# Four chained attention layers: values of two layers from one product, weights turned in one piece, output in quadrants

## The reference, cut to what matters

```
# layer 1, decay
w = exp(-exp(time_decay + tanh(xw @ td_w1) @ td_w2))        # td_w1: 256x64, td_w2: 64x256
# layer 2
v      = h_lojban @ w_v.T                                    # context
probs  = softmax(q @ k.T / sqrt(256))
x2     = x1 + alpha * (probs @ v) @ w_o.T
# layer 3
v      = encoder_hidden_state @ Wv + bv                      # the same context, 64 columns
out    = softmax(scores) @ v
```

## Time and profile before

| | |
|---|---|
| median of 3 runs | 1621.43 us (1621.12 to 1624.65) |
| span of the profiled execution | 1618.4 us |
| outside the span, against the median | 3.0 us |
| TensorE, VectorE, ScalarE, GpSimd busy | 88%, 67%, 38%, 39% |
| one full iteration | 92.4 to 92.9 us, a few of them 94 to 96 |

### The profile page before, as it was taken

One profiled execution on the slowest core, in us unless ns is written; L12 is line 12 of the kernel. 1 busy time (PEld: TensorE's weight loads), 2 busy tenths in 40 slices (PEclk: granted clock), 3 DMA queues, 4 the chain that ended last, 5 costly groups with the idle time before them and its releaser, 6 DMA issues.

```text
span 1618.4 us, 34489 instructions
## 1 busy us (share of the span) xinstructions
PE 1416.4 (88%) x14312; PEld 1073.0 (66%) x14312; DVE 1076.6 (67%) x2073; ACT 622.2 (38%) x1351; POOL 626.3 (39%) x604
## 2 busy tenths in 40 slices
PE   5878999999999999999999999999999999987664
PEld 4656777666777776666777766667777667765443
DVE  2354686866768686776868677686868667774735
ACT  2333444334334443434444443444443343432221
POOL 1061615336261634526162543616153352605210
PEclk9898999999999999999999999999999999997786
DMA  7030313114031312304041221403131130404000
GB/s 288 11 56 14 57 31 46 39 24 71 17 57 31 53 33 33 60 17 63 25 63 31 40 44 23 72 17 57 32 45 40 29 65 17 54 4 57 3 11 7
DMA packets 65787, 70.40 MB, mean 43 GB/s; under 512 B 19808, under 2 KB 54752, under 8 KB 65248
## 3 DMA queue, kind: packets, MB, share of 16 engines
q1 hardware_dynamic: 65632, 68.19, 22.1%
HBM read 30.42 MB, written 4.19 MB: 21 GB/s over the span
## 4 chain that ended last, share of the span: by engine, by line
PE 61%; DVE 15%; ACT 8%; POOL 6%; issue 4%; DMA 4%; SPq 1%; DVEq 0%; POOLq 0%; ACTq 0%
PE pw L411 13%; PE pw L389 12%; PE pw L591 7%; PE pw L597 7%; PE pw L447 4%; PE pw L542 4%; DMA big<-kvrg 4%; PE pw L495 3%; DVE c L1096 3%; PE pw L395 2%; ACT ptA L814 2%; PE pw L400 2%; POOL ab L1039 2%; DVE ab L1250 2%; POOL ab L1003 1%
## 5 line engine op out<-in xcount | busy, mean ns | idle before, releaser
L1250 DVE TENSOR_TENSOR_SCAN ab<-pw,ab 128x256 f32<-128x256 f32 x256 | 160.4, 674 | 107.0 <-ACT ab L924 81.3
L1003 POOL TENSOR_TENSOR ab<-big,kvrg 128x504 f32<-128x504 f32 x128 | 161.5, 1262 | 74.3 <-DMA big<-kvrg 50.9
L1039 POOL TENSOR_TENSOR ab<-ab,kvrg 128x512 f32<-128x512 f32 x128 | 167.7, 1315 | 0.5 <-DVE ab L1250 0.5
L988 POOL TENSOR_TENSOR vtmp_B<-mv_B,eps 128x2 f32<-128x2 f32 x16 | 3.1, 197 | 383.7 <-DVE mv_B L1111 383.7
L1026 POOL TENSOR_TENSOR big<-big,xaB 128x512 f32<-128x512 f32 x80 | 93.3, 1175 | 99.8 <-DVE big L1229 99.8
L389 PE MATMUL pw<-big,wb 128*128 128x256 f32 x512 | 127.8, 393 | 0.2 <-ACT kvrg L897 0.2
L591 PE MATMUL pw<-tA,wb 128*128 128x256 f32 x512 | 125.5, 396 | 2.1 <-DVE tA L1194 2.1
L1229 DVE SCALAR_TENSOR_TENSOR big<-pw,wa,sxB 128x256 f32<-128x256 f32 x160 | 67.0, 478 | 78.1 <-PE pw L495 78.1
L816 ACT ACTIVATE ptC<-pw 128x1024 f32<-128x1024 f32 x64 | 62.1, 1022 | 146.8 <-PE pw L447 146.8
L597 PE MATMUL pw<-wb,ptA 128*128 128x256 f32 x512 | 115.6, 379 | 0.0
L591 PEld LDWEIGHTS pw<-tA,wb 128*128 128x128 f32 x512 | 97.9, 196 | 25.0 <-issue 9.3
(11 more groups left out here) (211 smaller groups left out, 3096.8 us busy)
## 6 DMA issues: line engine op xcount, KB each, us to landing
big<-kvrg SPq DMA_DIRECT2D x256, 128.0 KB, 3.9
hT<-in_h SPq DMA_DIRECT2D x16, 512.0 KB, 4.1
wb<-in_wb SPq DMA_DIRECT2D x1, 5120.0 KB, 21.2
a<-in_x SPq DMA_DIRECT2D x16, 256.0 KB, 2.7
xB<-in_x SPq DMA_DIRECT2D x16, 256.0 KB, 2.7
result<-c SPq DMA_DIRECT2D x16, 256.0 KB, 2.0
m<-in_mask SPq DMA_DIRECT2D x16, 128.0 KB, 2.5
m<-in_amask SPq DMA_DIRECT2D x32, 64.0 KB, 2.3
```

Of the source, the lines that this page charges most:

```text
L1003: G.tensor_tensor(ab[i % 4][:, :, :, 1:S], vx[i % 3].rearrange("p j (b s) -> p j b s", b=NB)[:, :, :, 0:S - 1], k, ALU.mult).then_inc(kv_p ...
L1039: G.tensor_tensor(ab[i % 4][:, :, :, :], st[i % 2][:, :, :, :], r, ALU.mult).then_inc(pd_ok, 1)
L1250: last = V.tensor_tensor_scan(st[i % 2][:, j, :, :].rearrange("p b s -> p (b s)"), kn(b5)[:, i // 4, :], ab[i % 4][:, j, :, :].rearrange(" ...
```

## The change

Three edits.

1. `v3` is no longer a stage. `m_vo` is 64 columns wider and carries layer 3's value weights; `l2v` makes 320 columns for each sequence, into two banks (sequences 0 and 2 or 1 and 3 in one), and ScalarE copies both to `uS`. VectorE takes layer 3's values out of `uS` (SBUF) into `v3s`, in eight pieces as before, but at stage `l2v`, so ahead of `fv`. The load of the next context moves from `v3` to `k3`.
2. `l2p` is one transpose of 128x128; `l2o` takes weights and values of token tile c from partitions 64c on, writes sequence e of it to partitions 64e on, and each token tile to a bank of its own.
3. `td2` is stored twice with 128 rows (once in the upper half, once in the lower, zeros elsewhere); `pw1`'s tanh is one instruction of 128 rows, and `pw2` is four products of 128 rows and 128 columns.

```diff
-ORDER = "ABABBABBBABBABBCBABBABBBBBCACBCBBBCCABBCCACBCBBBCAAACBBBBCABCBACAABCAABBCACCCACCC"
+ORDER = "ABABBABBBABBABBCBABBABBBBBCACBCBBBCCABBCCACBCBBBCAAABBBBCABCBACAABCAABBCACCCACCC"
...
-USES = {... "l2v": 1, ... "l2o": 1, "k3": 1, "v3": 1, ...}
+USES = {... "l2v": 2, ... "l2o": 2, "k3": 1, ...}
...
@@ TensorE
                 elif name == "pw2":
                     for m in range(2):
-                        last = mm(kn(b5)[:, m, :], w("td2")[0:64, m * P:(m + 1) * P], thB[0:64, 0, :], start=True, stop=True)
+                        for c in range(TT):
+                            last = mm(kn(b5)[:, m, tok(c)], w("td2", c)[:, m * P:(m + 1) * P], thB[:, 0, 0:P], start=True, stop=True)
...
                 elif name == "l2v":
-                    for b in range(NB):
-                        g = slice(64 * (b % 2), 64 * (b % 2) + 64)
+                    for kk in (k, k + 1):
+                        if kk > k and kk >= FIRST_FREE:
+                            pe.wait_ge(*spare(kk))
                         for c in range(2):
-                            last = mm(kn(bank(k))[g, b // 2, :], hT[t % 3][:, c, b, 0:S], m_vo[:, c, :], start=(c == 0), stop=(c == 1))
-                    last.then_inc(full(k)[0], 1)
+                            for h in range(2):
+                                last = mm(bank(kk)[64 * h:64 * h + 64, 0:C + 64], hT[t % 3][:, c, 2 * h + kk % 2, 0:S], m_vo[:, c, :],
+                                          start=(c == 0), stop=(c == 1))
+                        last.then_inc(full(kk)[0], 1)
...
                 elif name == "l2p":
-                    for c in range(TT):
-                        for e in range(2):
-                            g = slice(64 * e, 64 * e + 64)
-                            last = mm(bank(k)[g, c * S:(c + 1) * S], pbd[g, c, :], ident[g, g], start=True, stop=True)
-                    last.then_inc(full(k)[0], 1)
+                    nc.tensor.transpose(bank(k)[:, 0:P], pbd.rearrange("p t n -> p (t n)"), ident).then_inc(full(k)[0], 1)
                 elif name == "l2o":
+                    pe.wait_ge(*spare(k + 1))
...
                     for c in range(TT):
+                        g = slice(64 * c, 64 * c + 64)
                         for e in range(2):
-                            g = slice(64 * e, 64 * e + 64)
-                            last = mm(kn(bank(k))[g, c, :], ptb[g, c, :], uS[g, c, :], start=True, stop=True)
-                    last.then_inc(full(k)[0], 1)
+                            last = mm(bank(k + c)[64 * e:64 * e + 64, 0:C], ptb[g, e, :], uS[g, e, 0:C], start=True, stop=True)
+                        last.then_inc(full(k + c)[0], 1)
...
@@ ScalarE
                 elif name == "l2v":
-                    A(flat(uS), bank(k)[:, :], ACT.Copy).then_inc(read(k)[0], 2)
+                    for kk in (k, k + 1):
+                        if kk > k:
+                            act.wait_ge(*full(kk))
+                        A(uS[:, kk % 2, :], bank(kk)[:, 0:C + 64], ACT.Copy).then_inc(read(kk)[0], 2)
...
@@ VectorE
-                elif name == "v3":
-                    k = SLOT[name, i, t]
-                    dve.wait_ge(*full(k))
-
+                elif name == "l2v":
+                    dve.wait_ge(*read(SLOT[name, i, t]))
+                    dve.wait_ge(*read(SLOT[name, i, t] + 1))
                     for e in range(2):
                         for h in range(2):
                             for v in range(2):
                                 o = (2 * v + e) * W3
-                                last = V.tensor_copy(v3[64 * e:64 * e + 64, h:NB:2, :, v, o:o + W3],
-                                                     bank(k)[64 * h:64 * h + 64, 0:P].rearrange("p (b r x) -> p b r x", b=2, r=2)[:, :, :, o:o + W3])
-                    last.then_inc(read(k)[0], 2)
+                                last = V.tensor_copy(v3[64 * e:64 * e + 64, 2 * h:2 * h + 2, :, v, o:o + W3],
+                                                     uS[64 * h:64 * h + 64, :, C:C + 64].rearrange("p b (r x) -> p b r x", r=2)[:, :, :, o:o + W3])
+                    last.then_inc(v3_ok, 1)
...
@@ VectorE, once
-                V.tensor_scalar(flat(m_vo[:, :, :]), b5[:, :], vec("alpha"), None, ALU.mult).then_inc(set_m, 1)
+                V.tensor_copy(m_vo[:, :, C:C + 64], w("v3").rearrange("p (k n) -> p k n", k=2))
+                V.tensor_scalar(m_vo[:, :, 0:C], kn(b5), vec("alpha"), None, ALU.mult).then_inc(set_m, 1)
```

More of the change, by code:

```diff
@@ L36 @@
 WEIGHTS_B = [("w1", 2 * HID), ("w2", 8 * C),
-             ("m1", 2 * 160), ("m2", 2 * C), ("td1", 2 * 64), ("td2", C),
+             ("m1", 2 * 160), ("m2", 2 * C), ("td1", 2 * 64), ("td2", 2 * C),
              ("wk", 2 * C), ("wv", 2 * C), ("wr", 2 * C), ("wg", 2 * C), ("wo", 2 * C),
@@ L74 @@
     + [("gnorm", 0), ("gnorm", 1), ("gnorm", 2), ("gnorm", 3), ("gturn", 0), ("outg", 0), ("norm2", 0)],
-    "C": [(n, 0) for n in ("cturn", "fk", "l2k", "fr", "l2v", "fv", "x2turn", "l2s", "l2p", "l2o", "k3", "v3", "x3turn", "q3")]
+    "C": [(n, 0) for n in ("cturn", "fk", "l2k", "fr", "l2v", "fv", "x2turn", "l2s", "l2p", "l2o", "k3", "x3turn", "q3")]
     + attention(1) + [("norm3", 0)],
@@ L78 @@
 AHEAD = {"A": 2, "B": 1, "C": 0}
-ORDER = "ABABBABBBABBABBCBABBABBBBBCACBCBBBCCABBCCACBCBBBCAAACBBBBCABCBACAABCAABBCACCCACCC"
-USES = {"q0": 1, "k0": 2, "v0": 2, "out0": 1, "zturn": 2, "up": 1, "down": 1, "cturn": 2, "fk": 1, "l2k": 1, "fr": 1, "l2v": 1, "fv": 1,
-        "x2turn": 1, "l2s": 1, "l2p": 1, "l2o": 1, "k3": 1, "v3": 1, "x3turn": 1, "q3": 1, "out1": 1}
+ORDER = "ABABBABBBABBABBCBABBABBBBBCACBCBBBCCABBCCACBCBBBCAAABBBBCABCBACAABCAABBCACCCACCC"
+USES = {"q0": 1, "k0": 2, "v0": 2, "out0": 1, "zturn": 2, "up": 1, "down": 1, "cturn": 2, "fk": 1, "l2k": 1, "fr": 1, "l2v": 2, "fv": 1,
+        "x2turn": 1, "l2s": 1, "l2p": 1, "l2o": 2, "k3": 1, "x3turn": 1, "q3": 1, "out1": 1}
 RING = 2
@@ L164, in build @@
         m_qk = sb("m_qk", [P, 2, C])
-        m_vo = sb("m_vo", [P, 2, C])
+        m_vo = sb("m_vo", [P, 2, C + 64])
         qb0m = sb("qb0m", [P, 2, 2])
@@ L226, in build @@
         c3 = sb("c3", [P, TT, C])
-        fkS, kkS, gC, tS, uS, thC = (ptC[:, 512 * i:512 * (i + 1)].rearrange("p (k n) -> p k n", k=2) for i in range(6))
+        fkS, kkS, gC, tS, thC = (ptC[:, 512 * i:512 * (i + 1)].rearrange("p (k n) -> p k n", k=2) for i in (0, 1, 2, 3, 6))
+        uS = ptC[:, 2048:2048 + 2 * (C + 64)].rearrange("p (k n) -> p k n", k=2)
         pbd, ptb = (ptC[:, 3584 + 128 * i:3712 + 128 * i].rearrange("p (t n) -> p t n", t=TT) for i in range(2))
@@ L303, in build @@
         gn_d, gn_p, gt_ps, gt_sb, og_ok, og_ps = sem("gn_d"), sem("gn_p"), sem("gt_ps"), sem("gt_sb"), sem("og_ok"), sem("og_ps")
-        kk_ok, ff_d, l2_mx = sem("kk_ok"), sem("ff_d"), sem("l2_mx")
+        kk_ok, ff_d, l2_mx, v3_ok = sem("kk_ok"), sem("ff_d"), sem("l2_mx"), sem("v3_ok")
         fin_ok = sem("fin_ok")
@@ L354, in stage @@
                     load_x(t + 2, xB[t % 2], ld_x4[t % 2])
-                elif name == "v3" and t + 3 < TILES:
-                    sp.wait_ge(*full(SLOT["v3", 0, t]))
+                elif name == "k3" and t + 3 < TILES:
+                    sp.wait_ge(*full(SLOT["k3", 0, t]))
                     load_context(t + 3)
@@ L721, in part_c @@
                         pe.wait_ge(*read(SLOT["l2o", 0, t]))
+                        pe.wait_ge(*read(SLOT["l2o", 0, t] + 1))
                     for c in range(2):
@@ L735, in part_c @@
                     pe.wait_ge(*read(SLOT["l2s", 0, t]))
-                    for c in range(TT):
-                        for e in range(2):
-                            g = slice(64 * e, 64 * e + 64)
-                            last = mm(bank(k)[g, c * S:(c + 1) * S], pbd[g, c, :], ident[g, g], start=True, stop=True)
-                    last.then_inc(full(k)[0], 1)
+                    nc.tensor.transpose(bank(k)[:, 0:P], pbd.rearrange("p t n -> p (t n)"), ident).then_inc(full(k)[0], 1)
                 elif name == "l2o":
+                    pe.wait_ge(*spare(k + 1))
                     pe.wait_ge(*read(SLOT["l2p", 0, t]))
                     pe.wait_ge(*read(SLOT["l2v", 0, t]))
+                    pe.wait_ge(*read(SLOT["l2v", 0, t] + 1))
                     for c in range(TT):
+                        g = slice(64 * c, 64 * c + 64)
                         for e in range(2):
-                            g = slice(64 * e, 64 * e + 64)
-                            last = mm(kn(bank(k))[g, c, :], ptb[g, c, :], uS[g, c, :], start=True, stop=True)
-                    last.then_inc(full(k)[0], 1)
+                            last = mm(bank(k + c)[64 * e:64 * e + 64, 0:C], ptb[g, e, :], uS[g, e, 0:C], start=True, stop=True)
+                        last.then_inc(full(k + c)[0], 1)
                 elif name == "k3":
@@ L780, in part_c @@
                     pe.wait_ge(e_sb, 4 * TURN[1, t] + 3 + i)
-                    pe.wait_ge(*read(SLOT["v3", 0, t]))
+                    if i == 0:
```

(20 more changed lines are left out.)

## The result

The changed kernel takes 1655.35 us in the median of 4 runs (1653.43 to 1661.18), against 1621.28 before: **ratio 1.0221, 95% interval 1.019 to 1.0251: slower**, by about 2%; whether by more or less than that the interval leaves open. The forecast was 1649, range 1609 to 1667. A ratio leaves out executions that took over 1.5% more than the fastest of the same kernel, at a lower granted clock (three in run 5, one in run 8); the medians and spreads keep them.

What follows compares the result with a forecast made beforehand. TensorE's own work was taken as the chain for some 70 of 92.5 us. Terms -5.9 + 24.9 + 8.8 + 1.0 - 1.2 + 0.2 = +27.8 on 1618.4, plus 3.0 outside: 1649 us, range 1609 to 1667.

Steps and rivals of the forecast that it cites:

- The copies: VectorE, ahead of fv: SBUF copies wait for GpSimd, c2 done at 757.31 for 753.89, TensorE stands still 2.2 us.
- rival A: The SBUF copies ahead of fv don't use the port shared with GpSimd: faster, 1612 us; chance 20%.
- rival B: VectorE's c2 comes before GpSimd's next outer: 0.4 us late per iteration, pw2 pays for it, 1622 us; chance 8%.
- The shift per iteration: VectorE's L1318 and what follows it move 1.78 us later in each of 14 full iterations: +24.9 us.
- The clock: TensorE's granted clock falls after its standing still around x2turn, in 8 of 14 iterations: +8.8 us, bounds 0 and 15.
- The tile that I took as my example: At 942.31 the scores take 1.15 for 0.70 us, the clock at 1.2 GHz after TensorE stood still twice.
- the iteration without A: There c2 meets GpSimd's outer too (+2.1 us), and l2p and l2o are in the chain (-1.1): +1.0 us.
- the last: Last iteration, no GpSimd work: l2v costs 0.43, l2p and l2o save 0.9, x3turn's copy comes earlier: -1.2 us.
- Decay: pw2 on TensorE: 0.37 us saved (bounds 0 and 0.45) in each of 16 tiles, -5.9 us.
- `l2v`: TensorE, between the exponentials and sum 1: 320 columns for 256 cost +0.43 us, within 0.92 to spare, so 0.
- `l2p`, `l2o`: TensorE: l2p saves 0.15 us, l2o takes 0.6 for 1.05 with four quadrants at once; neither matters in a full iteration.
- The shared product: Dropping v3's products (0.5 us, plus 0.30 of waiting) and copies (1.20) gives 0.1 us per iteration, no more.

Runs made afterwards that it cites:

- run 5: Kernel before with decay's part alone (td2 stored twice, one tanh, pw2 over 128 rows): 1621.23 us, ratio 0.9993.
- run 8: Kernel before with decay's and second attention's parts, v3 still a stage with its PSUM source: 1613.46 us, ratio 0.997.
- Run 2: Changed kernel with the eight copies at the same place, each as a maximum over an axis of length one: 1610.42 us, ratio 0.9971.
- run 7: Kernel before with only eight copies from uS into an unread tile added on VectorE ahead of fv: 1662.18 us, ratio 1.0268.
- Run 4: Changed kernel with four unread products of 256 columns on TensorE ahead of x2turn's wait for c2: 1640.5 us, ratio 1.0164.
- run 1: Changed kernel with VectorE's eight copies moved from ahead of fv to behind oturn 1: 1607.74 us, ratio 0.9945.
- run 6: Kernel before with second attention's part alone (l2p one transpose, l2o in quadrants and two banks): 1616.45 us, ratio 0.9992.
- run 9: Changed kernel with copies behind oturn 1, plus unread products in three idle stretches of TensorE: 1605.39 us, ratio 0.9911.

## Why the prediction was right

**The copies.** The step held in its mechanism and nearly in every time. Forecast and measured, from the end of scan 4: copies done +2.87 and +2.93; c2 done +4.93 and +4.92; wait before `x2turn` 2.2 and 2.12; in an iteration without a clock fall (the one at 389 us) L1322 starts +10.96, forecast +11.07. Which copies would wait was a little off: the first and the third, not the first and the second; one small copy slipped in between two of GpSimd's instructions. That changed little, since the end of the product sets when the rest can run. Run 2 excludes the place alone (rival A's cheap copies are what it made), run 7 excludes the other edits as the cause of the loss, and rival B's wash did not come: c2 missed the gap by 0.6 us.

**The shift per iteration.** I had +1.78 with +1.41 left after decay's gain. Iterations without a clock fall are 93.9 to 94.0, +1.5. In 14 of them some 21 us, forecast 19.7.

**The clock, the term with the least behind it.** I put 1.1 on 8 of 14 iterations, +8.8. A fall at the scores costs 95.1 - 93.95 = 1.15, as forecast, but in the profiled execution there were eleven (12.7 us), and I had left out both the falls at `mix2` (3 after for 1 before; an iteration with both kinds takes 98.4, so 98.4 - 93.95 - 1.15 = 3.3 each, 9.9) and what the kernel before already lost: its 14 distances take 1303.0 us, 8.6 over 14 x 92.46, 7.0 of it in the three with a fall (96.00, 94.31 and 94.07). In all the clock term of the two profiled executions is 12.7 + 9.9 - 7.0 = 15.6, forecast 8.8. Run 4 shows the first part by removing it; that the additional falls at `mix2` come from the change is not shown, a single execution being too few. Nor is 15.6 the term of the median: the other three executions after are 4.3 to 7.8 us shorter at a higher granted clock. If the clock is all of that difference, it is some 10 in the median (an estimate: 15.6 less the 5.9 between 1659.4 and the median of the four spans), and 8.8 was near, in part by luck.

The tile that I took as my example was also misread. The kernel before has two such tiles, and how long TensorE had waited for `sum` 1 does not part them from the rest: it was 1.32 us at 940 and 1.02 at 1312, where the clock fell, and 1.19 at 1034, where it did not (timeline of TensorE before):

```profile
1034.47 0.64 PE L411 MATMUL pw<-ab,wb 128*32 128x256 f32 x8 [1.19 <-POOL ab L1039]
1036.49 0.70 PE L731 MATMUL pw<-ptC,tC 128*64 128x64 f32 x16 [0.80 <-issue]
...
1312.04 0.64 PE L411 MATMUL pw<-ab,wb 128*32 128x256 f32 x8 [1.02 <-POOL ab L1039]
1314.06 0.96 PE L731 MATMUL pw<-ptC,tC 128*64 128x64 f32 x16 [0.79 <-issue]
```

What decides in which iteration the clock falls stays open.

**Where the 41.0 us of the two profiled executions lie.** Up to the first `l2v` +0.6 (forecast -0.5); the 14 full iterations +37.6 (21 of waiting, 15.6 of clock, 1 unexplained; forecast 28.5); the iteration without A +3.1 (forecast +1.0; the clock was low for 30.7 of its 69.7 us, before for 23.9 of 66.6); the last -0.3 (forecast -1.2: `l2o` and the earlier `x3turn` save, but TensorE ran at 1.2 GHz for 41 of 59.0 us, before for 34 of 59.3). Outside the span lie 1.8 us after, for the 3.0 that I had carried over. The forecast's +27.8 is 6.3 under the 34.1 of the medians; with the clock term near, that would be these smaller terms, each about 1 to 2 us too low. No trace of a median execution shows it.

**The other parts.** Decay: 0.34 by run 5's rows, 0.37 forecast. `l2v`: +0.37 on TensorE (764.06 to 766.36, for 1.93 before; forecast 0.43), hidden, as run 1 shows. `l2p`, `l2o`: the four quadrants run at once and it is worth nothing in a full iteration (run 6), as worked out. The shared product: 0.25 per iteration by the profiled executions, under-priced at 0.1. Rival A's 1612 against a before of 1621.4 is a ratio of 0.994; run 1 has 0.9945.

## What to carry to other kernels

Before moving the source of small VectorE copies from PSUM to SBUF, look at what GpSimd does at that time: each may wait until GpSimd's current instruction ends, and what is queued behind it on VectorE pays. If one must stand there, a form such as a maximum over an axis of one element took the same place at 1.1 us for eight in place of 3.0. When a change adds a stall of two microseconds on TensorE, price also the work behind it at half the clock; here a few useless products in the stall took most of that price away (run 4).

## What the runs showed of the hardware

- A reduction over an axis of length one, SBUF to SBUF, was never seen to wait for GpSimd (0 of 128 over 0.2 us, run 2); the copy of the same elements at the same place took over 1 us in 28 of 128.
- Four 64x64 quadrants with 256 columns each, different data and two banks, ran at once: 0.66 us for 1.08 with two.
- At the scores the clock fell to 1.2 GHz in 11 of 14 full iterations, behind two idle stretches of 2.12 and 0.79 us with 0.6 of work between; the other three had the same two stretches. With 2.0 us of useless products in the first (L725, run 4) it fell there in none.
- The 12 executions of run 5's kernel spread from 1606 to 1643 us, with the mean granted clock going from 0.969 to 0.941. The six of run 9, with the stretches filled, spread from 1600.6 to 1607.5; but the six of run 1, with nothing filled, from 1603.7 to 1608.3, so a narrower spread by the filling is not shown.
